# Audio tower on one core: new orders of the segments on all five engines, and a hinted back branch of the main loop

## The chip, the cores and the metric

One core of one Trainium2 chip runs the whole kernel. The metric is the device time of one execution in microseconds (us), lower is better. The kernel before takes 8142.36 us, the median of 3 executions (8140.66 to 8146.43).

## What is computed

For each of 32 sequences of 80,000 samples, the samples are padded and cut into L = 626 frames of 128, and five residual steps follow. All is float32.

```python
h = dct(frames(x))                                  # 626 x 128 per sequence
h = h + mamba_both_ways(layernorm(h))               # scan over time, forward and backward
h = h + moe(layernorm(h))                           # 8 experts, top 2, 128 -> 512 -> 128, gelu
h = h + window_attention(layernorm(h))              # 8 heads of 16, window of 8
h = h + pattern_ffn(layernorm(h))                   # three top-k layers:
#   a1 = gelu(u @ input_patterns.T)   keep top 64 of 512
#   a2 = gelu(kept @ process_in.T)    keep top 128 of 256, softmax, weigh process_values
#   a3 = gelu(agg @ output_in.T)      keep top 64 of 512, weigh output_patterns
```

## The kernel before

**Tiles and stages.** The 626 frames of a sequence are padded to 640, five tiles of 128 partitions. The work is cut into four stages. Stage 1 is the DCT, the first layer norm and the two Mamba directions; stage 2 the mixture of experts; stage 3 the windowed attention; stage 4 the three top-k layers and the output. The stages are pipelined over sequences: while stage 1 works on sequence b, stage 2 works on b-1, stage 3 on b-2 and stage 4 on b-3 (STAGE_LAG).

**The order of the work.** Each engine (TensorE = PE, ScalarE = ACT, VectorE = DVE, GpSimd = POOL, SyncE = SP, which issues DMAs) has a Python generator for each stage, which yields after each segment of instructions. `merged` (L109 to L115) walks a string of digits and emits the next segment of the stage that the digit names. The five strings PE_ORDER, ACT_ORDER, DVE_ORDER, POOL_ORDER and SP_ORDER (L97 to L106) thus fix, by hand, in which order an engine interleaves the four stages:

```python
for digit in order:
    stage = stages[int(digit) - 1]
    if stage is not None:
        next(stage, None)
```

Engines meet through counting semaphores. A segment that waits holds up all that stands behind it on its own engine, of whatever stage. `run` (L353 to L361) emits three ramp-up passes, one hardware loop `engine.Fori(last, NB)` (L358) of 29 iterations whose body is one pass of all four stages, and three ramp-down passes. The loop's branch back is taken 28 times on each engine.

**Stage 1 in the code.** PE transposes x and h, projects the normalized u in 20 half units (L565, into PSUM pS; dA at L562), and for each of 12 units (6 chunks of 105 frames in 2 directions) mixes: C against B (L576), x against its decay (L583), and combines the result with Mt (L593, L599). ACT applies silu to the projections (L847 to L855: Bw, Cs, xs, zs). DVE computes dt (L1046 to L1063), scans the decays (L1071, ab), weighs (L1079 Xw, L1082 Mt), and ends with the variance (L1093) and the scaling of the two directions' outputs into ub_t (L1101). Layer norm moments are L1030 to L1036 on DVE; POOL applies them (L382 rstd, L387 u).

**Stage 2 in the code.** DVE picks the experts (L1114 to L1134) and counts each token's slot (L1139 to L1150). POOL scatters un by slot to routed_rows (L439, L441), SP brings back the rows in 17 tiles of 128 slots. Per tile PE turns the rows (L662), multiplies up (L674, four matmuls) and down (L683, L685), ACT copies the turned rows (L920), applies gelu (L907, four activations), issues the load of a later tile's expert weights (L887) and the store of the answers (L893). POOL gathers the answers (L447, L449), DVE adds them to h (L1157, L1160).

**Stage 3 in the code.** PE q, k, v (L716), DVE products of shifted q and k (L1173 to L1179), ACT exp (L950), POOL and DVE weigh and sum the window by trees of two-input instructions over 128x640 (POOL L459 to L488; DVE L1184, L1188, L1191), and DVE adds to h (L1194, L1198).

**Stage 4 in the code.** POOL copies h into hk (L496). PE computes a1 (L746), transposes the kept (L753, selT), a2 (L761), and so on to the last product (L795, pD); ACT applies gelu (a2 at L970) and copies selT (L967). DVE takes the top 64 of 512 by rounds of MAX8 and MATCH_REPLACE8 (`take_top`, L1218, L1221, closed by L1229), and sorts a2's pairs of halves for the top 128 of 256 (`split_pairs`: L1240 to L1243, then rounds of L1248 and L1251, closed by L1254, L1255; `weigh_pairs` L1265 to L1275). DVE adds the result to hk (L1280); SP stores it (L344, L345).

## Time and profile before

| | before |
|---|---|
| median of 3 executions | 8142.36 us (8140.66 to 8146.43) |
| the profiled execution | 8142.98 us |
| its span in the trace | 8141.2 us |
| granted TensorE clock, mean of the span (share of full speed) | 0.800 |
| DVE busy | 6959.1 us (85% of the span) |
| PE busy | 5529.4 us (68%) |
| ACT, POOL busy | 3232.6 us (40%), 3040.7 us (37%) |
| mean DMA rate | 69 GB/s |

The profiled execution took 8142.98 us, of which the trace's span covers 8141.2 us; it stands 0.62 us above the median. Busy shares are averages over the ramps and the 29 iterations; the iterations repeat closely, so that one of them, read from the loop's first DVE instruction to the next, can be looked at in the place of all.

### The profile page before, as it was taken

To read this page: it belongs to the slowest core of one execution; us is meant where nothing else is said; L and a number is where in the kernel's file an instruction comes from. 1 tells how busy PE (TensorE), PEld (TensorE's weight loads), DVE (VectorE), ACT (ScalarE), POOL (GpSimd) and SP (SyncE) were. 2 spreads that over 40 slices of the span, in tenths; PEclk is the share of its full clock that TensorE was granted. 3 is DMA by queue.
4 is the path that set the end of the run, shared out by engine and by line. 5 is a ranking of instruction groups with operands and counts; after the bars stand their busy time and mean duration, and the time that the engine had idled before them with its cause. 6 is when DMAs were issued, how large, how long until landed. Compare 5 with 4: busy or idle time off the path is not lost.

```text
span 8141.2 us, 109594 instructions
## 1 busy us (share of the span) xinstructions
PE 5529.4 (68%) x31240; PEld 4441.6 (55%) x31240; DVE 6959.1 (85%) x22124; ACT 3232.6 (40%) x7204; POOL 3040.7 (37%) x3192
## 2 busy tenths in 40 slices
PE   6766677776667767667767667767667767667433
PEld 5655555555555555556555556555556555556322
DVE  2378989888989888989888989888989888989887
ACT  2343444433444443344443344433344443344311
POOL 2344443334443433443333443333443333443320
PEclk8887788878788888788877788878788878778755
DMA  2322222222222222222221222222222222222200
GB/s 71 107 79 62 66 85 78 74 65 60 65 85 79 78 62 61 62 85 81 79 64 57 62 84 82 80 62 62 64 77 82 81 65 65 67 67 82 69 2 3
DMA packets 342763, 561.90 MB, mean 69 GB/s; under 512 B 33728, under 2 KB 261792, under 8 KB 341664
## 3 DMA queue, kind: packets, MB, share of 16 engines
q10 hardware_dynamic: 152576, 357.68, 14.2%
q1 hardware_dynamic: 168992, 153.83, 7.3%
q0 software_dynamic: 20480, 41.98, 1.7%
q8 instruction: 311, 5.10, 0.3%
q14 instruction: 404, 3.31, 0.1%
HBM read 484.63 MB, written 68.74 MB: 68 GB/s over the span
## 4 chain that ended last, share of the span: by engine, by line
DVE 67%; PE 9%; issue 8%; DMA 5%; POOL 5%; ACT 3%; ACTq 2%; SPq 1%; DVEq 0%; POOLq 0%
DVE m L1218 15%; DVE work L1221 9%; DVE work L1251 7%; DVE sorted L1248 6%; DVE a L1221 4%; DVE ab L1071 3%; DMA rows<-routed_rows 3%; DVE lg L1173 2%; PE pS L565 2%; PE pD L761 2%; DVE Mt L1082 2%; DMA decay_rows<-dAT 2%; POOL u L387 2%; DVE stats L1030 2%; DVE red L1188 2%
## 5 line engine op out<-in xcount | busy, mean ns | idle before, releaser
L1218 DVE MAX8 m<-work 128x8 f32<-128x512 f32 x1792 | 1143.4, 678 | 1.0
L1221 DVE MATCH_REPLACE8 work<-m,work 128x512 f32<-128x512 f32 x1536 | 1024.8, 674 | 0.0
L565 PE MATMUL pS<-u_fm,wconv_s 128*128 128x315 f32 x3072 | 929.0, 457 | 6.1 <-ACT Cs L849 5.8
L674 PE MATMUL pM<-turned,expert 128*128 128x128 f32 x4352 | 655.2, 297 | 331.7 <-ACT turned L920 327.4
L674 PEld LDWEIGHTS pM<-turned,expert 128*128 128x128 f32 x4352 | 586.0, 206 | 423.6 <-issue 359.9
L565 PEld LDWEIGHTS pS<-u_fm,wconv_s 128*128 128x128 f32 x3072 | 614.2, 205 | 256.3 <-issue 52.8
L907 ACT ACTIVATE hid<-pM,expert 128x128 f32<-128x128 f32 x2176 | 621.2, 370 | 331.6 <-PE pM L674 330.2
L459 POOL TENSOR_TENSOR lg<-lg,red 128x640 f32<-128x640 f32 x256 | 388.5, 1557 | 920.2 <-DVE red L1179 920.2
L685 PE MATMUL pM<-expert,hid 128*128 128x128 f32 x4352 | 672.9, 306 | 0.0
L685 PEld LDWEIGHTS pM<-expert,hid 128*128 128x128 f32 x4352 | 631.6, 223 | 0.0
L599 PE MATMUL pS<-Mt,Xw 121*64 121x121 f32 x3072 | 294.2, 321 | 488.7 <-DVE Mt L1082 486.4
L1251 DVE MATCH_REPLACE8 work<-sorted,work 128x128 f32<-128x128 f32 x2240 | 590.7, 274 | 0.0
L1248 DVE MAX8 sorted<-work 128x8 f32<-128x128 f32 x2560 | 541.0, 277 | 1.1
L1218 DVE MAX8 m<-a 128x8 f32<-128x512 f32 x768 | 503.4, 676 | 40.2 <-issue 34.7
L488 POOL TENSOR_TENSOR lg<-lg 128x640 f32<-128x640 f32 x224 | 363.5, 1647 | 429.7 <-DVE lg L1184 424.7
L1071 DVE TENSOR_TENSOR_SCAN ab<-ab,cst 121x488 f32<-121x488 f32 x384 | 485.1, 1270 | 36.8 <-DMA ab<-decay_rows 36.7
L599 PEld LDWEIGHTS pS<-Mt,Xw 121*64 121x64 f32 x3072 | 189.2, 160 | 585.7 <-DVE Mt L1082 532.9
L998 ACT COPY selT<-pD 128x512 f32<-128x512 f32 x160 | 93.6, 585 | 999.6 <-PE pD L790 999.6
L410 POOL TENSOR_TENSOR yg<-xs,zs 128x525 f32<-128x525 f32 (+1 forms) x256 | 195.3, 796 | 771.6 <-ACT xs L862 763.1
L465 POOL TENSOR_TENSOR red<-lg 128x640 f32<-128x640 f32 x128 | 197.4, 1580 | 741.8 <-ACT lg L950 741.8
L920 ACT COPY turned<-pM 128x256 f32<-128x256 f32 (+1 forms) x544 | 196.2, 361 | 681.9 <-PE pM L685 330.5
L382 POOL TENSOR_TENSOR rstd<-vare,mhalf 128x5 f32<-128x5 f32 x160 | 187.1, 1170 | 624.8 <-DVE vare L1036 624.8
(243 smaller groups left out, 13975.1 us busy)
## 6 DMA issues: line engine op xcount, KB each, us to landing
expert<-in_experts ACTq DMA_DIRECT2D x544, 578.0 KB, 3.9
ab<-decay_rows SPq DMA_DIRECT2D x384, 230.7 KB
rows<-routed_rows SPq DMA_DIRECT2D x128, 256.0 KB, 5.1
answer_rows<-turned ACTq DMA_DIRECT2D x256, 128.0 KB, 4.0
x_sb<-in_x SPq DMA_DIRECT2D x32, 256.0 KB
out<-hk SPq DMA_DIRECT2D x32, 256.0 KB
routed_rows<-un,slot POOLq DMA_INDIRECT x320, 2.8
rows<-answer_rows,slot POOLq DMA_INDIRECT x320, 2.6
```

Of the source, the lines that this page charges most:

```text
L459: last = nc.gpsimd.tensor_tensor(lg[:, w, :], lg[:, w, :], red[:, 0, :], ALU.subtract)
L488: last = nc.gpsimd.tensor_tensor(lg[:, w, :], lg[:, w, :], lg[:, w + n, :], ALU.add)
L565: last = nc.tensor.matmul(pS[:, 512 * (n % 3):512 * (n % 3) + HQ], wt, tap(d, i, half * HQ, HQ), start=(j == 0), stop=(j == len(blocks) - 1))
L599: last = nc.tensor.matmul(pS[r * HD:(r + 1) * HD, B2 + g * WIN:B2 + (g + 1) * WIN], Xw[d][:, hh, :], Mt[d][:, hh, :], start=False, stop=(g ...
L674: last = nc.tensor.matmul(pM[:, bank(i) + j * P:bank(i) + (j + 1) * P], w1_of(i, j), turned[:, (i + 2) % 4, 1, :], start=True, stop=True)
L685: last = nc.tensor.matmul(at, hid[:, i % 2, j, :], w2_of(i, j), start=False, stop=(j == KB - 1))
L907: last = nc.scalar.activation(hid[:, i % 2, j, :], pM[:, at:at + P], ACT.Gelu, bias=b1_of(i, j))
L1071: nc.vector.tensor_tensor_scan(decays, decays, c("scan_src", WIN), 0.0, ALU.mult, ALU.add).then_inc(G["scanned"].s, 1)
L1218: link(nc.vector.max(m8[:, i, :], now[i]), len(tiles) - 1)
L1221: link(nc.vector.match_replace(work[i], m8[:, i, :], now[i], GONE), len(tiles) - 1)
L1248: link(nc.vector.max(top[:, 8 * r:8 * r + 8], left), 2 * n - 1)
L1251: link(nc.vector.match_replace(left, top[:, 8 * r:8 * r + 8], left, GONE), 2 * n - 1)
```

## The change

The five strings of orders are replaced by others with the same count of each digit per string, so no segment is added, dropped or changed, and each engine only takes them in another sequence. The loop is built with a hint of its back branch on each engine: the loop body of each engine begins with one more instruction, which names the branch at its end.

```diff
--- before.py
+++ after.py
@@ -94,16 +94,16 @@
 
 
 
-PE_ORDER = ("14444143433323231111111111214141411134411111111111122424322112211114111111114111112242222122211221211221"
-            "114221111111112114211411112444241414112241111211144142114221412112244144143414434433")
-ACT_ORDER = ("44414334413233121111111113114141421111111111341111424223242112111111111111112424222224224422132221241212"
-             "14424214442144424122144244122421221114424144433")
-DVE_ORDER = ("34244414244211114442444444444434444444411111144444444441111111111433111411114444144444444434444441414343"
-             "42")
-POOL_ORDER = ("321421333333331121113314")
-
-
-SP_ORDER = ("1112221111111213443")
+PE_ORDER = ("44441414112131211114334321111143111131444111111311111341111121122211244212121212211121141111211111212122"
+            "111221121212121211412414114141114211411144142112242424111421212421442144144314344433")
+ACT_ORDER = ("44444111421231413131411131111134111411141411131131231111121124241122212111214211212421244132122221221222"
+             "44144242411444244122424124421222421444124114433")
+DVE_ORDER = ("43441442444141211424424444444414134444144411111444414441144411111411113134414144414444443444444444314344"
+             "12")
+POOL_ORDER = ("123233333331311421331141")
+
+
+SP_ORDER = ("1131221112111213144")
 
 
 def merged(order, *stages):
@@ -355,7 +355,7 @@
             last = max(STAGE_LAG)
             for i in range(last):
                 merged(order, *[stage(engine, i - lag) if i >= lag else None for stage, lag in zip(stages, STAGE_LAG)])
-            with engine.Fori(last, NB) as b:
+            with nc.Fori(last, NB, engines=[engine.engine], hint_back_edge=True) as b:
                 merged(order, *[stage(engine, b - lag) for stage, lag in zip(stages, STAGE_LAG)])
             for i in range(NB, NB + last):
                 merged(order, *[stage(engine, i - lag) if i - lag < NB else None for stage, lag in zip(stages, STAGE_LAG)])
```

**TensorE, the third product a2 of a sequence (L761) and the routed rows (L662).** L761 is stage 4's product of the kept activations selT, in steps of four matmuls; L662 turns stage 2's rows when their DMA has landed; L565 is a projection of stage 1. Before:

```order
L565 MATMUL pS<-u_fm,wconv_s 128x315 x4
L557 REGISTER_ALU
L565 MATMUL pS<-u_fm,wconv_s 128x315 x4
L557 REGISTER_ALU
L565 MATMUL pS<-u_fm,wconv_s 128x315 x4
L661 ISA
L662 MATMUL pM<-cst,rows 128x128 x2
L761 MATMUL pD<-cst,selT 128x256 x4
```

In the change:

```order
L557 REGISTER_ALU
L565 MATMUL pS<-u_fm,cst 128x315
L761 MATMUL pD<-cst,selT 128x256 x4
L753 MATMUL pD<-cst,a 128x128 x4
L761 MATMUL pD<-cst,selT 128x256 x4
L557 REGISTER_ALU
L560 REGISTER_ALU
L562 MATMUL pS<-cst,dtA 128x121
L565 MATMUL pS<-u_fm,cst 128x315
```

The third L761 stood behind the first L662 of a sequence; now the third one stands among projections, ahead of L562 and 25 rows ahead of the first L662.

**TensorE, the first mix of the scan (L576, L583).** L565 is the projection, L674 to L685 is one expert tile of stage 2. Before:

```order
L565 MATMUL pS<-u_fm,cst 128x315
L557 REGISTER_ALU
L565 MATMUL pS<-u_fm,cst 128x315
L557 REGISTER_ALU
L565 MATMUL pS<-u_fm,cst 128x315
L557 REGISTER_ALU
L565 MATMUL pS<-u_fm,cst 128x315
L753 MATMUL pD<-cst,a 128x128 x4
L604 REGISTER_ALU
L576 MATMUL pS<-Cs,Bw 128x121
L583 MATMUL pS<-cst,xs 128x128 x2
```

In the change:

```order
L661 ISA
L662 MATMUL pM<-cst,rows 128x128
L557 REGISTER_ALU
L565 MATMUL pS<-u_fm,cst 128x315
L674 MATMUL pM<-turned,expert 128x128 x4
L681 REGISTER_ALU
L683 MATMUL pM<-expert,cst 128x128
L685 MATMUL pM<-expert,hid 128x128 x4
L662 MATMUL pM<-cst,rows 128x128
L604 REGISTER_ALU
L576 MATMUL pS<-Cs,Bw 128x121
L583 MATMUL pS<-cst,xs 128x128 x2
```

The first mix had three tiles' ups (L674) between the first L662 and itself, and four projections just ahead of it; now it has five, and the last projection stands between two of them.

**VectorE, the end of the loop body.** L1101 scales the scan's output, L1198 ends the attention's residual, L1280 adds stage 4's result to hk, L1157 adds the gathered answers. Before:

```order
L1229 SCALAR_TENSOR_TENSOR a<-a,m 128x512 x2
L1101 SCALAR_TENSOR_TENSOR ub_t<-pS,rstd,ub_t 128x128 x10
L1030 BN_STATS stats<-ub_t 128x6 x5
L1033 BN_AGGR mv<-stats 128x2 x5
L1035 TENSOR_SCALAR nmean<-mv 128x5
L1036 TENSOR_SCALAR vare<-mv 128x5
L1104 ISA
L1194 TENSOR_TENSOR h<-h,pA 128x512
L1279 REGISTER_ALU
L1280 TENSOR_TENSOR hk<-hk,pD 128x128
L1197 REGISTER_ALU
L1198 TENSOR_TENSOR h<-h,pA 128x128
```

In the change:

```order
L1201 ISA
L1279 REGISTER_ALU
L1280 TENSOR_TENSOR hk<-hk,pD 128x128 x2
L1309 ISA
L1101 SCALAR_TENSOR_TENSOR ub_t<-pS,rstd,ub_t 128x128 x10
L1030 BN_STATS stats<-ub_t 128x6 x5
L1033 BN_AGGR mv<-stats 128x2 x5
L1035 TENSOR_SCALAR nmean<-mv 128x5
L1036 TENSOR_SCALAR vare<-mv 128x5
L1104 ISA
L1153 ISA
L1157 SCALAR_TENSOR_TENSOR h<-rows,top,h 128x128 x5
```

L1101 and the moments of ub_t stood ahead of L1194, L1198 and both last L1280; now they stand behind them, just ahead of L1157. On GpSimd the end of the body changes with them: it ended u of ub_t (L382, L387, L424, L427), u of h (L382, L387), hk (L496), h (L431), and now ends u of h, hk (L496), u of ub_t, h (L431).

## Rows read from the trace of the kernel before

**Rows 1.** The page: busy time of the engines; the chain that ended last.
```profile
PE 5529.4 (68%) x31240; PEld 4441.6 (55%) x31240; DVE 6959.1 (85%) x22124; ACT 3232.6 (40%) x7204; POOL 3040.7 (37%) x3192
...
DVE 67%; PE 9%; issue 8%; DMA 5%; POOL 5%; ACT 3%; ACTq 2%; SPq 1%; DVEq 0%; POOLq 0%
```

**Rows 2.** Windows, one iteration: us, busy PE, PEld, DVE, ACT, POOL, clock, DMA, GB/s.
```profile
3164.90:3407.30 242.40, 169.73 (x976) 137.56 (x976) 217.19 (x692) 101.58 (x225) 94.76 (x99) 0.82 0.25 72
```

**Rows 3.** DVE's waits in that iteration: total us, times, longest.
```profile
DVE work L1240 <- ACT a L970: 8.2, 1, 8.2
DVE h L1157 <- POOL hk L496: 6.2, 1, 6.2
DVE stats L1030 <- issue: 3.6, 2, 2.3
DVE Xw L1079 <- PE pS L583: 2.0, 3, 0.9
```

**Rows 4.** DVE's timeline at the loop's head: start, us, then [idle before <- releaser].
```profile
3167.20 0.87 DVE L1030 BATCH_NORM_STATS2 stats<-h 128x6 f32<-128x128 f32 x4 [2.25 <-issue]
3169.47 0.29 DVE L1030 BATCH_NORM_STATS2 stats<-h 128x6 f32<-128x128 f32 x1 [1.39 <-issue]
```

**Rows 5.** Timeline around the third a2, PE and DVE.
```profile
3237.07 0.69 PE L662 MATMUL pM<-cst,rows 128*128 128x128 f32 x2 [6.95 <-DMA rows<-routed_rows]
3237.55 3.62 PE L761 MATMUL pD<-cst,selT 128*128 128x256 f32 x8
...
3241.69 0.56 DVE L1240 TENSOR_TENSOR work<-a 128x384 f32<-128x384 f32 x1 [8.17 <-ACT a L970]
```

**Rows 6.** DVE's timeline: last slot, one sort round of six lists, the first Xw.
```profile
3213.09 0.17 DVE L1150 CAST slot<-slot_f 128x10 int32<-128x10 f32 x1
...
3272.13 1.25 DVE L1248 MAX8 sorted<-work 128x8 f32<-128x128 f32 x6
...
3274.85 1.25 DVE L1248 MAX8 sorted<-work 128x8 f32<-128x128 f32 x6
...
3278.97 0.40 DVE L1079 TENSOR_TENSOR Xw<-pS,dts 121x256 f32<-121x256 f32 x1
```

**Rows 7.** ACT's timeline: a table load, the last silu of the projections, two later tiles' gelu.
```profile
3248.14 1.28 ACT L907 ACT_TABLE_LOAD   x1
...
3256.08 2.03 ACT L855 ACTIVATE zs<-pS 128x315 f32<-128x315 f32 x4 [1.74 <-PE pS L565]
...
3323.18 1.15 ACT L907 ACTIVATE hid<-pM,expert 128x128 f32<-128x128 f32 x4
...
3330.70 1.14 ACT L907 ACTIVATE hid<-pM,expert 128x128 f32<-128x128 f32 x4 [0.72 <-PE pM L674]
```

**Rows 8.** Timeline of the loop's tail, DVE and POOL, and the program's last L1280.
```profile
3146.13 2.80 DVE L1101 SCALAR_TENSOR_TENSOR ub_t<-pS,rstd,ub_t 128x128 f32<-128x128 f32 x10
...
3151.33 0.28 DVE L1280 TENSOR_TENSOR hk<-hk,pD 128x128 f32<-128x128 f32 x1
...
3155.59 0.29 DVE L1280 TENSOR_TENSOR hk<-hk,pD 128x128 f32<-128x128 f32 x1 [1.46 <-PE pD L795]
...
3160.77 1.25 POOL L496 TENSOR_TENSOR hk<-h,zero 128x640 f32<-128x640 f32 x1
...
3162.11 1.14 DVE L1157 SCALAR_TENSOR_TENSOR h<-rows,top,h 128x128 f32<-128x128 f32 x4 [6.23 <-POOL hk L496]
...
8137.68 0.29 DVE L1280 TENSOR_TENSOR hk<-hk,pD 128x128 f32<-128x128 f32 x1 [3.96 <-PE pD L795]
```

**Rows 9.** DVE instructions with two SBUF inputs beside POOL's: timeline, and L1071's min/median/max ns.
```profile
3302.89 1.52 DVE L1254 SCALAR_TENSOR_TENSOR work<-sorted 128x130 f32<-128x130 f32 x1
...
3328.72 2.15 DVE L1071 TENSOR_TENSOR_SCAN ab<-ab,cst 121x488 f32<-121x488 f32 x1
...
L1071 DVE TENSOR_TENSOR_SCAN ab<-ab,cst x384: 1147/1167/2445, 72.1 to 7470.2; 121x488 f32<-121x488 f32 x192
```

**Rows 10.** POOL's timeline: the answers have landed, the gathers can start.
```profile
3369.34 0.19 POOL L447 TENSOR_TENSOR ticks<-zero 128x1 f32<-128x1 f32 x1 [6.25 <-DMA answer_rows<-turned]
```

## The prediction

> **What bounds the kernel now.** I read the page first, then one iteration of the loop. Of the five engines DVE is by far the busiest, 6959.1 us or 85%, with PE next at 68%, and DVE holds 67% of the chain that ended last [rows 1]. An iteration takes 242.40 us, in which DVE is busy 217.19 and PE 169.73 [rows 2]. So the iteration is DVE's instructions plus DVE's waits; an engine other than DVE counts only where DVE waits for it. The list of DVE's waits is therefore the list of what a new order can win: 8.2 us at L1240, 6.2 at L1157, 3.6 at the loop's head under "issue", 2.0 in three pieces at L1079 [rows 3], and 1.5 at L1280 [rows 8]. What each waits for:
>
> L1240 needs the third a2 of stage 4. Its product L761 began at 3237.55, right behind L662, for which PE had stood idle 6.95 us until the routed rows had landed; L761 then took 3.62 us and L1240 began at 3241.69 [rows 5]. A DMA of stage 2 held up stage 4, by nothing but order.
>
> L1157 stands behind hk (L496) on GpSimd, which began at 3160.77 and took 1.25 [rows 8]; hk is free when the last L1280 has been done and stored. The head's 2.25 and 1.39 have no releaser [rows 4]: DVE just passed its branch, so I read them as instructions being fetched.
>
> **The change, part by part.** In each iteration, gains positive. DVE's instructions are the same ones, but for one hint, so only waits and contention can move.
>
> *L1240.* All three L761 now stand ahead of L562 and so of L662. Stage 4's input is there early, since the second L761 was done before the projections ended. The third a2 is then ready before DVE comes to L1240: +8.2.
>
> *The first Xw (L1079).* It is the price of that order. Before, DVE came to it at 3278.97, 111.8 us behind the head at 3167.20 [rows 4, 6]. Off that go the waits ahead of it (8.2 and the head's second 1.4, with 0.3 of small ones): 101.9 of work. In the new DVE order three sort rounds with their closing instructions, which stood ahead of the first scan, stand behind it: a round of six lists takes 3274.85 - 3272.13 = 2.72 [rows 6], so two of those and a shorter one, 7.4 in all. DVE comes to the first Xw at 94.5. When is the product (L583) there? The last slot is cast 3213.09 + 0.17 - 3167.20 = 46.1 behind the head, 44.4 without the waits; two sort rounds of the other group of lists are moved ahead of it (an estimate of 2.5 each, by the same rows), so 49.4. The rows landed 3237.07 - 3213.26 = 23.8 later [rows 5, 6]: 73.2. The first mix now stands behind five ups and four downs of expert tiles, against three and two. On ACT, which alternates gelu and silu, the last four zs ended at 3256.08 + 2.03, 21.0 behind the rows [rows 5, 7]. In the new order ACT has between the rows and its last silu five sets of gelu at 1.14, eight table loads at 1.28, four zs at 0.5 [rows 7], and some fifteen copies, silus and DMA issues of 0.2 to 0.6: 5.7 + 10.2 + 2.0 + 7.3 = 25.2, and some 4 of waits for PE's ups, an estimate by the gap ahead of the second gelu row (0.72 a tile) [rows 7]. That is 29.1, so the product comes at 102.3 and DVE waits 102.3 - 94.5 = 7.8. Bounds: 4 if ACT never waits for PE, 12 if each of four tiles loses another microsecond. I take 7.8: -7.8.
>
> *The back edge.* The hint adds one instruction to each engine's body. Nothing in this trace has a hint, so its price is bounded by the head's rows: from nothing won to all 3.6 won [rows 3]. I take 3.4, near the upper end, because 2.25 and 1.39 are idle time with no releaser that only a late instruction stream explains [rows 4]. The Trainium skill ("Runtime: NRT & Kernel Launch", on instruction fetch mechanics) says that prefetch is purely sequential and a taken branch beyond the pages held forces a fetch; by that rule the 3.6 stays, which is a rival below. +3.4.
>
> *The tail.* Time from the start of L1101 at 3146.13, S, which is when the last selection is done. Before, L1157 began at S + 16.0, with 6.23 + 1.46 of waits in it [rows 8]. In the change L1194, L1093, L1198 and the moments of h come first, and L1280 at S + 3.5. Its second piece came 4.26 behind the first in this row (3155.59 against 3151.33), and waited 3.96 where nothing stood between, at the program's end [rows 8]: S + 7.8, done at S + 8.1. L1101 (2.80) and the moments (1.9) now cover what follows, and L1157 could begin at S + 12.85. hk: at the program's end 8137.97 to 8141.2, 3.2 us, is the store of the last piece; then L496 takes 1.25 [rows 8]: S + 12.6. It is in time. Waits of 7.7 become 4.0: +3.7. If L496 ended as long behind L1280 as now (3162.0 - 3155.9 = 6.1), it would be S + 14.2 and the gain 2.3.
>
> *L1079's small waits.* 2.0 in three [rows 3], where scans follow each other closely. The new DVE order puts rounds between some of them: 2.0 to 0.5, +1.5. Stage 4's softmax, though, now stands behind one more set of gelu on ACT, for which L1265 waits about a third of 1.14 [rows 7]: -0.4.
>
> *Contention.* L1254 on 128x130 took 1.52 us, where a two-input L1280 on 128x128 takes 0.28 [rows 8, 9], and one L1071 took 2.15 where its median is 1.167 [rows 9]; in both cases GpSimd was in a two-input instruction over 128x640 of the attention's trees. That is 2.2 us, of which the new orders part rather over half, by where they put those trees: +1.2, between nothing and 2.2. The Trainium skill ("SBUF — State Buffer", who interferes with whom) says that VectorE with two SBUF inputs and GpSimd reading SBUF exclude each other, whoever came first. The rows agree in direction; by the rule all 2.2 would go only if no pair met at all.
>
> *What is hidden.* The gathers (L447) began 3369.34 - 3167.20 = 202.1 behind the head, 132.3 behind the rows [rows 5, 10]. With the same distance they begin at 205.5 and end their ten issues some 13.6 later, at 219. S lies 3146.13 + 242.40 - 3167.20 = 221.3 behind the head now [rows 2, 4, 8], some 218 in the change. Behind the gathers GpSimd still has u of h, which must start by about S + 6 = 224 for L496 to end in time. That is 5 us of slack, 7 if the tiles go a little faster. Input loads, decay rows and POOL's L382/L387 move within slack larger than that; I cost them at nothing, and the gathers are the first cover that would go.
>
> **Sum.** 8.2 - 7.8 + 3.4 + 3.7 + 1.5 - 0.4 + 1.2 = 9.8 us an iteration, 232.6 instead of 242.4. Times 29 it is 284. The profiled execution took 8142.98, so 7858.8; the median lies 0.6 lower, so 7858. The ramps hold pieces of the same orders, which I put at nothing, within 10 us either way.
>
> **Rivals.**
>
> *B, the first Xw doesn't wait.* If ACT gets its silus done between the tiles, or the rows land sooner, 7.8 come back: 17.6 an iteration, 8142.4 - 510 = 7632. For it: ACT is only 101.58 us busy of 242.40 [rows 2]. Against it: the table loads between gelu and silu, and PE's order, which puts the last projection behind the fourth up. Chance 0.10.
>
> *C, the hint does nothing.* By the rule named above, or because the idle is something else: 6.4 an iteration, 7956. Chance 0.15.
>
> *D, slower.* Expert tiles that share PE with projections and mixes don't go at 5 us each: later tiles began their gelu at 3323.18 and 3330.70, 7.5 apart [rows 7]. With the first gelu 5.2 behind the rows and four tiles at 7.5, the last silu comes at 73.2 + 5.2 + 30 + 2.0 = 110.4, and the first Xw waits 15.9: of 9.8 there remain 1.7. If besides the twelve further tiles each lose 1 us, 12 in all, the gathers pass their slack of 7 by 5, and L1157 waits 5 again: -3.3 an iteration, 8238. It decides from a first wait of 17.6, or from gathers more than 8.7 late. Against it: PE is free for 72 of 242 us [rows 2]. Chance 0.07.
>
> *E, the edits cancel* (the first wait near 17): 8142, chance 0.03.
>
> **Numbers.** Forecast 0.65, B 0.10, C 0.15, D 0.07, E 0.03. The range takes in C, and the forecast's own bounds: a first wait of 4 gives 7748, one of 12 gives 7980, a tail of 2.3 and no contention won 7934. 7740 to 8005 leaves out B, D and E, 0.20. About 0.2% (16 us) is what a measurement can tell here from no change: faster 0.90, same 0.03, slower 0.07.
>
> **What would show it.** DVE's waits of one iteration should read: no L1240; a wait at the first L1079 for PE L583 of 4 to 12 us; "issue" at the head under 0.5; L1280 near 4 and L1157 near nothing; the iteration 232.6. If "issue" still reads 3.6, the hint's term is wrong; if L1157 waits for a DMA of the rows, D's gathers are late; if the first L1079 shows no wait, it is B. DVE busy should be 216.0 in the iteration. The forecast as a whole is wrong if DVE waits more than 18 us in it, or if a line that isn't named here holds over 3.

## The result: 8208 us against 8142, slower by 0.8%

The changed kernel takes 8208.41 us, the median of 4 executions (8200.29 to 8213.67), against 8141.51 (8130.08 to 8146.43) of the kernel before beside it: ratio 1.0083, 95% interval 1.0066 to 1.0101. The forecast was 7858, faster. Nor was it the rival that stood for slower.

The profiled execution took 8208.12 us, span 8206.2, mean granted clock 0.801 (before 0.800). From the page of the profile after, engines' busy time and the chain that ended last, to be read against [rows 1]:

```profile
PE 5716.2 (70%) x31240; PEld 4562.0 (56%) x31240; DVE 7055.1 (86%) x22124; ACT 3365.3 (41%) x7326; POOL 2989.4 (36%) x3192
...
DVE 41%; PE 27%; ACT 16%; issue 8%; POOL 4%; ACTq 2%; DMA 1%; DVEq 0%; SPq 0%; POOLq 0%
```

DVE runs the same 22,124 instructions and is busy 96 us longer. The chain has left it: 67% of it lay on DVE, now 41%, and PE and ACT hold 43%. ACT has 122 more table loads. One iteration, from the head of DVE's loop body to the next, in the windows view (columns as in [rows 2]) and in the list of DVE's waits (total us, times, longest):

```profile
3181.86:3427.64 245.78, 178.46 (x976) 143.17 (x976) 220.37 (x692) 105.97 (x230) 93.09 (x100) 0.81 0.24 70
```

```profile
DVE Xw L1079 <- PE pS L583: 13.4, 2, 12.5
DVE hk L1280 <- PE pD L795: 4.0, 1, 4.0
DVE ab L1071 <- DMA ab<-decay_rows: 2.1, 1, 2.1
DVE a L1265 <- ACT a L983: 1.7, 2, 1.5
DVE lg L1173 <- ACT v L947: 0.8, 1, 0.8
DVE h L1198 <- PE pA L726: 0.5, 1, 0.5
```

Against [rows 3], every wait that the change was to remove is gone: L1240, L1157 and the head's "issue". In their place stands one of 12.5 us at the first L1079. Line by line, gains positive, with the forecast's term behind each:

| us in an iteration | measured | forecast |
|---|---|---|
| L1240 | +8.2 | +8.2 |
| the loop's head | +3.6 | +3.4 |
| the tail: L1157 +6.2, L1280 -2.5 | +3.7 | +3.7 |
| the first L1079 | -12.5 | -7.8 |
| the other L1079 | +1.1 | +1.5 |
| L1265 | -1.7 | -0.4 |
| DVE's busy time (contention) | -3.2 | +1.2 |
| the first scan, L1071, for its decay rows | -2.1 | none |
| L1173 -0.8, small ones +0.3 | -0.5 | none |
| sum | -3.4 | +9.8 |

-3.4 is 242.40 - 245.78. Of the 13.2 us between the two sums, 4.7 are the first L1079, 4.4 the contention, 1.3 L1265, and 2.6 waits for which the forecast had no term; small differences make up the rest. Times 29, -3.4 would be 98 us, and the spans differ by 65.0 (8206.2 and 8141.2): the ramps, and iterations a little unlike these two, gave back some 33, where the forecast had put the ramps at nothing within 10.

**Where the first L1079 lost 4.7.** The slots came exactly when forecast: the last cast ended at 3231.61, 49.4 behind the head at 3182.18. The rows' DMA was issued at 3249.30 and took 7.2 us before (3229.88 to 3237.07), so the rows were there at about 3256.5. Timelines of PE, ACT and DVE, changed kernel:

```profile
3257.84 4.51 PE L565 MATMUL pS<-u_fm,wconv_s 128*128 128x315 f32 x16 [1.11 <-ACT Cs L849]
3262.19 0.27 PE L662 MATMUL pM<-cst,rows 128*128 128x128 f32 x1
```

```profile
3249.53 0.42 ACT L947 COPY v<-pA 128x320 f32<-128x320 f32 x1
3254.80 1.37 ACTq L887 DMA_DIRECT2D expert<-in_experts  x3
3256.29 0.42 ACT L947 COPY v<-pA 128x320 f32<-128x320 f32 x1 [6.34 <-issue]
3262.50 0.27 ACT L925 COPY turned<-pM 128x128 f32<-128x128 f32 x1 [3.75 <-PE pM L662]
```

```profile
3292.06 0.42 DVE L1079 TENSOR_TENSOR Xw<-pS,dts 121x256 f32<-121x256 f32 x1 [12.46 <-PE pS L583]
```

PE did not wait for the rows any more. It came to the first L662 at 3262.19, some 6 us after them. Most of that is PE's own work. The windows from the head to the first L662, before and after (columns as in [rows 2]), show it:

```profile
3167.20:3237.07 69.87, 49.56 (x205) 34.87 (x203) 63.28 (x202) 28.86 (x51) 21.90 (x33) 0.84 0.19 57
3182.18:3262.19 80.01, 59.38 (x237) 43.65 (x238) 75.76 (x233) 31.55 (x54) 25.61 (x38) 0.81 0.17 50
```

PE was busy 9.8 us longer there, since the new order puts more projections (L565) and all three L761 ahead of L662. Without its wait for the rows it would have come 62.9 us behind the head before, and it came at 80.0 now; the other 7 us are waits for GpSimd and ACT (L533 for u, 3.51, is the largest new one). ACT, too, had stood 6.34 us with no releaser: it reads the 17 experts' numbers into registers (L350) and issues three loads. Before, the same segment came early (4.96 us, behind projection 4). But of those 6.34 only 1.11 reached PE, in its wait for Cs (L849); ACT in its turn then waited 3.75 us for PE's L662. From L662 on, the forecast's count holds: the last silu ended 29.1 us behind it, 29.1 was forecast, with the forecast's eight table loads and five sets of gelu. The exact match is in part luck, since ACT's three largest waits in it come to 7.3 us where the forecast had some 4, and its copies to less. The forecast started those 29.1 at the landing of the rows, 73.2 behind the head; they started at 80.0. So the product came 7.6 us later than forecast (109.9 for 102.3), and DVE came to it 2.9 later too (97.4 for 94.5), which leaves the 4.7.

**Where DVE's busy time grew.** Timeline of the changed kernel, DVE, ACT and POOL:

```profile
3311.82 1.68 DVE L1240 TENSOR_TENSOR work<-a 128x256 f32<-128x256 f32 x1
3313.43 1.80 DVE L1241 TENSOR_TENSOR work<-a 128x256 f32<-128x256 f32 x1
3315.26 1.56 DVE L1242 TENSOR_SCALAR work<-work 128x256 f32<-128x256 f32 x1
3316.86 0.42 DVE L1243 TENSOR_REDUCE nmax<-work 128x2 f32<-128x256 f32 x1
```

```profile
3306.99 1.86 DVE L1265 TENSOR_TENSOR_SCAN a<-minus,a 128x256 f32<-128x256 f32 x3 [1.51 <-ACT a L983]
3307.11 4.47 ACT L950 ACTIVATE lg<-lg 128x5120 f32<-128x5120 f32 x1
3311.65 6.61 POOL L465 TENSOR_TENSOR red<-lg 128x640 f32<-128x640 f32 x4 [30.85 <-ACT lg L950]
```

The first three took 0.40, 0.42 and 0.29 us before, on the same shapes; now each takes about as long as one of GpSimd's four instructions beside them (6.61 / 4 = 1.65). The meeting comes from ACT's order. ACT's squares (L983) end at 3306.96. DVE waits for them at L1265 and comes to its second L1240 4.9 us later. ACT takes the attention's exponentials (L950) almost straight behind them, and GpSimd, which waits for those, starts 4.7 us behind the squares. So one event starts both engines, 0.17 us apart at the meeting. Over the run the three lines cost 117 us more, and L1254 34 us less, as the change meant it to. The reduction behind them is not slowed.

### The profile page after: what moved, and what is told of

Same layout as the page of the kernel before. It is cut to its first block, busy times and chain, and to the rows that moved or that the text cites. A ratio compares the mean times of both kernels' runs of the same rounds, so it can differ in the third digit from the quotient of the medians.

```text
span 8206.2 us, 109861 instructions
## 1 busy us (share of the span) xinstructions
PE 5716.2 (70%) x31240; PEld 4562.0 (56%) x31240; DVE 7055.1 (86%) x22124; ACT 3365.3 (41%) x7326; POOL 2989.4 (36%) x3192
## 4 chain that ended last, share of the span: by engine, by line
DVE 41%; PE 27%; ACT 16%; issue 8%; POOL 4%; ACTq 2%; DMA 1%; DVEq 0%; SPq 0%; POOLq 0%
DVE m L1218 12%; PE pS L565 9%; DVE work L1221 8%; PE pD L761 3%; DVE a L1221 3%; PE pM L674 3%; PE pM L685 3%; ACT L907 2%; ACT hid L907 2%; ACT L855 2%; DVE stats L1030 2%; PE pD L795 2%; DVE work L1251 2%; ACTq L887 1%; DVE sorted L1248 1%
## 5 line engine op out<-in xcount | busy, mean ns | idle before, releaser
L1218 DVE MAX8 m<-work 128x8 f32<-128x512 f32 x1792 | 1144.5, 680 | 0.0
L674 PE MATMUL pM<-turned,expert 128*128 128x128 f32 x4352 | 700.9, 314 | 416.1 <-ACT turned L920 413.0
L565 PE MATMUL pS<-u_fm,wconv_s 128*128 128x315 f32 x3072 | 922.3, 451 | 74.5 <-ACT Cs L849 74.5
L674 PEld LDWEIGHTS pM<-turned,expert 128*128 128x128 f32 x4352 | 621.7, 220 | 528.6 <-issue 497.9
L907 ACT ACTIVATE hid<-pM,expert 128x128 f32<-128x128 f32 x2176 | 620.7, 369 | 513.9 <-PE pM L674 511.7
L565 PEld LDWEIGHTS pS<-u_fm,wconv_s 128*128 128x128 f32 x3072 | 600.1, 200 | 330.3 <-ACT Cs L849 104.7
L685 PE MATMUL pM<-expert,hid 128*128 128x128 f32 x4352 | 725.8, 323 | 0.0
L685 PEld LDWEIGHTS pM<-expert,hid 128*128 128x128 f32 x4352 | 686.8, 240 | 0.0
L488 POOL TENSOR_TENSOR lg<-lg 128x640 f32<-128x640 f32 x224 | 340.6, 1545 | 736.1 <-DVE lg L1184 733.4
L1079 DVE TENSOR_TENSOR Xw<-pS,dts 121x256 f32<-121x256 f32 x384 | 157.7, 411 | 504.1 <-PE pS L583 504.1
L1071 DVE TENSOR_TENSOR_SCAN ab<-ab,cst 121x488 f32<-121x488 f32 x384 | 484.8, 1263 | 113.9 <-DMA ab<-decay_rows 113.9
L1218 DVE MAX8 m<-a 128x8 f32<-128x512 f32 x768 | 504.9, 678 | 32.6 <-issue 20.7
L599 PE MATMUL pS<-Mt,Xw 121*64 121x121 f32 x3072 | 271.1, 302 | 290.6 <-DVE Mt L1082 290.6
L998 ACT COPY selT<-pD 128x512 f32<-128x512 f32 x160 | 93.6, 585 | 919.8 <-PE pD L790 919.8
L761 PE MATMUL pD<-cst,selT 128*128 128x256 f32 x1280 | 390.2, 459 | 81.0 <-ACT selT L967 81.0
```

The source lines that it names most:

```text
L488: last = nc.gpsimd.tensor_tensor(lg[:, w, :], lg[:, w, :], lg[:, w + n, :], ALU.add)
L565: last = nc.tensor.matmul(pS[:, 512 * (n % 3):512 * (n % 3) + HQ], wt, tap(d, i, half * HQ, HQ), start=(j == 0), stop=(j == len(blocks) - 1))
L674: last = nc.tensor.matmul(pM[:, bank(i) + j * P:bank(i) + (j + 1) * P], w1_of(i, j), turned[:, (i + 2) % 4, 1, :], start=True, stop=True)
L685: last = nc.tensor.matmul(at, hid[:, i % 2, j, :], w2_of(i, j), start=False, stop=(j == KB - 1))
L761: last = nc.tensor.matmul(pD[:, 512:512 + NP_], selT[:, j * P:(j + 1) * P], pw[:, j, :], start=(j == 0), stop=(j == 3))
L907: last = nc.scalar.activation(hid[:, i % 2, j, :], pM[:, at:at + P], ACT.Gelu, bias=b1_of(i, j))
```

## Experiments

Orders are changed in them, and diffs show the segments of one engine in the sequence in which it takes them ("projection 17" is a half unit of L565, or its silu on ACT; "tile 0" the first expert tile). Each result is a ratio to the kernel before on the same chip, since chips differ: on the five other chips that the runs came to, before takes 8466 to 8517 us.

### The hint alone, and the orders alone

```diff
-            with engine.Fori(last, NB) as b:
+            with nc.Fori(last, NB, engines=[engine.engine], hint_back_edge=True) as b:
```

> The kernel before with the hint of the back branch on all engines and nothing else. Theory: the idle time at the head of VectorE's loop, 3.6 us an iteration, goes and nothing takes its place, so about 108 us less: 8035, 'issue' at L1030 gone. Rival: the wait moves to L1240 or L1157, which end on a DMA or on GpSimd: 8110 to 8141, with L1240 or L1157 longer by up to 3.6.

8409.19 us against 8512.86, ratio 0.9882 (0.9865 to 0.9898): 104 us won, 108 forecast. "Issue" at L1030 is gone and nothing took its place. The page of the profile shows the fetching too: its two queues of kind "instruction" moved 715 packets before and 493 with the hint, in the kernel before as in the changed one, about 8 fewer for each of the 28 branches back. Next, the changed kernel with that line undone:

> The changed kernel with the loop's back branch as it was, without the hint. Theory: the hint is worth the same in either order, so 8208 + 108 = 8316, and the orders alone are slower than before by some 175 us. Rival: in the new orders the first L1079 waits for ScalarE's chain, which absorbs VectorE's idle time at the head: 8208 to 8250, with a shorter wait at L1079.

8430.07, ratio 0.9899 (0.9882 to 0.9916). The orders alone were **faster** than before, where theory and rival had both expected slower. Either the hint costs something in the new orders, or the chip changes the verdict. Both kernels on one chip, the changed one and again the one without the hint:

> The changed kernel once more, beside the kernel before on this chip, because the earlier runs showed another time for the kernel before (8513 us) on another chip. Theory: the ratio belongs to the chip's delays outside the engines (register reads and instruction loading on ScalarE), so on a chip with 8513 for before the changed kernel takes about 8430 - 100 = 8330, ratio 0.98; on one with 8141, 8208, ratio 1.008. Rival: the ratio is the kernel's own, 1.008 everywhere.

> The changed kernel without the hint, the same kernel as before it under another label, beside the changed one on one chip. Theory: 100 us slower than the changed kernel with the hint. Rival: within 20 us of it, because the first L1079 waits for ScalarE anyway.

The changed kernel took 8317.84 against 8466.22, ratio 0.9819 (0.9802 to 0.9835); without the hint 8408.39, ratio 0.9930. So the hint is worth 91 us in the new orders too (85 of it at L1030), and the verdict on the change depends on the chip: 0.8% slower on the one of the result, 1.8% faster here.

### What differs between the chips

> The kernel before, unchanged, for a profile on this chip. Theory: where it takes 8460 to 8520 us instead of 8141, the difference lies in ScalarE, which stops 10 to 12 us without a releaser in each of the two stretches in which GpSimd issues indirect DMAs (L441, L449), and VectorE waits for it at L1240, L1280 and L1093. Rival: it lies in the engines' own busy time or in TensorE's clock.

8464.24 us. DVE's busy time is 6965.2 against 6959.1 [rows 1], so DVE is not slower. PE is busy 5709.8 against 5529.4, at a granted clock of 0.782 against 0.800. The clock is not what makes these chips slow: the changed kernel had 0.807 in after_again and took 110 us longer than on the chip of the result at 0.801. The fetching is not it either: the instruction queues moved the same 715 packets. DVE's waits in this run, and ACT's without a releaser ("remote": the semaphore changed at a moment when no recorded instruction or DMA ended):

```profile
DVE work L1240 <- ACT a L970: 321.2, 30, 13.0
DVE vare L1093 <- PE pS L627: 198.4, 32, 18.7
DVE h L1157 <- POOL hk L496: 192.9, 31, 8.0
DVE Xw L1079 <- PE pS L583: 154.0, 103, 20.9
DVE hk L1280 <- PE pD L795: 139.1, 61, 4.2
```

```profile
ACT xs L852 <- issue: 294.5, 31, 11.7
ACT selT L998 <- remote: 220.6, 26, 9.7
```

On the chip of the result L852 had 156.5 of it and L998 none. DVE's waits account for 310 of the 321 us between the two spans: 81 at L1240, 148 at L1093 and 81 at L1280. The stops end with GpSimd's indirect DMAs. In the changed kernel on such a chip ACT ends a square (L867) and then stands until the last gather is issued. Timelines of that run (after_again), ACT, the last gather of POOL, PE and DVE:

```profile
3444.14 2.43 ACT L867 ACTIVATE zs<-yg 128x1280 f32<-128x1280 f32 x2
3456.78 0.59 ACT L998 COPY selT<-pD 128x512 f32<-128x512 f32 x1 [10.21 <-remote]
```

```profile
3454.78 0.99 POOL L449 DMA_INDIRECT rows<-answer_rows,slot  x1 [0.30 <-issue]
```

```profile
3452.46 1.09 PE L790 MATMUL pD<-cst,a 128*128 128x128 f32 x4 [0.53 <-DVE a L1229]
3453.63 0.47 PE L726 MATMUL pA<-cst,kf 128*128 128x128 f32 x1
```

```profile
3455.36 0.17 DVE L1093 TENSOR_SCALAR vare<-pS 128x10 f32<-128x10 f32 x1 [1.79 <-remote]
3456.81 0.29 DVE L1198 TENSOR_TENSOR h<-h,pA 128x128 f32<-128x128 f32 x1 [1.29 <-remote]
```

ACT moves on 1.0 us behind the last gather's end (1.0 to 1.5 in 24 iterations). It does so because of a semaphore. L998 waits for L790 and DVE's L1198 for L726, both on PE; those matmuls had ended 3.2 and 2.7 us before, by the record, and both engines moved on 0.03 us apart. The trace keeps the times of the semaphores' updates: the one of the last L790 changed at 3456.76, the one of L726 at 3456.79. On the chip of the result each changed within 0.02 us of the recorded end. There ACT waits 7.34 us for the same L790, so of the 10.21 here only 2.9 are the stop. What comes late is the news that PE is done; ACT does not lack its own instructions at that place. With half as many gathers:

```diff
-            for k in range(2 * TILES):
+            for k in range(TILES):
                 nc.gpsimd.indirect_dma_start(rows[:, k, :], None, answers_d, ...
```

> The changed kernel with five gathers (L449) instead of ten, so that GpSimd's stretch of indirect DMAs lasts 6.5 instead of 13 us; it leaves out the answers of the second chosen expert, whose rows keep old data. Theory: on a slower chip ScalarE's stop at L998, which in the changed kernel lasted 10.2 us and ended 1.1 to 1.4 us behind the last gather, ends 6.5 us sooner and lasts some 4 us, again 1 to 2 us behind the last gather. Rival: the stop has nothing to do with the gathers and lasts 10 us.

```profile
ACT selT L998 <- PE pD L790: 920.0, 160, 19.1
```

L998 waits for PE alone, and DVE's L1093 waits 37.2 us in 3, as on the chip of the result (37.4 in 3). Theory and rival are not told apart by the length of the stop: five gathers end some 5 us before L790 does, so a stop that ends 1 to 2 us behind them is covered by the wait for PE. But nothing that ends late is left, and the kernel, without the second expert's answers and in one execution, took 8198.83 against 8470.73 of before, close to what the changed kernel takes on the chip of the result (8208). So what these chips charge the changed kernel hangs on the ten gathers. Why the updates come late there, why one chip has none of it, and whether recording them plays a part, stays open.

The same stops cost the kernel before more, and that gives the reversal: those chips charge the kernel before some 320 us and the changed one 110. At the gathers, L1093 rises by 148 us before and by 87 in the changed kernel, L1280 by 81 and 16. Before, L627, for which L1093 waits, stands behind the late ACT on PE. PE stood 4.97 us in the iteration looked at in before_look, and its granted clock was then 0.50, the lower level (1.2 GHz), for 9 us: the 40 matmuls of L627 took 8.53 us, against 4.71 on the chip of the result, at 0.90. In the new order L627 stands ahead of the last L790. At the scatters (L441), ACT's register reads took 9.5 us on those chips (294.5 in 31), or 11.3 (349.5 in 31, the run with the hint alone), instead of 5.0, worth 81 at L1240. In the changed kernel they lie behind the scatters, 6.5 (200.2 in 31) on the one chip and 6.8 (210.7 in 31) on the other.

### Single moves out of the change

The register reads put back among earlier projections:

```diff
 ACT
+register reads and three expert loads (L350, L887)
 projection 7 ... projection 10, kf, v
-register reads and three expert loads (L350, L887)
 v, projection 11
```

> The changed kernel with one segment of ScalarE moved ahead: the reading of the experts' registers with the first three loads of expert weights (L350, L887) stands before the silu of projection 7 instead of behind projection 10, other orders as changed. Theory: ScalarE loses some 5 us with it in either place, and behind projection 10 it falls right before the routed rows, so that TensorE comes 6 us late to the first L662; moved ahead, part of that hides in ScalarE's waits for TensorE: the first L1079 waits 8 to 10 instead of 12.5, 8070 to 8150. Rival: the wait is set by the alternation of gelu and silu over five expert tiles alone: L1079 waits 12 and more, 8200 or, if the third a2 is late now, 8230.

8561.67, ratio 1.0060 (1.0044 to 1.0077), against 0.98 of the changed kernel on such chips. Worse: the segment then lay in the scatters and took 8.7 us (270.3 in 31 stops at L855), L1240 waited again, 237.6 us in all, and L1079 still 455.7. So on such a chip that place is no better.

The third a2 alone, in the kernel before:

```diff
 PE, ACT
+third a2 (L761 on PE, L970 on ACT)
 first two L662 (L925 on ACT)
-third a2 (L761 on PE, L970 on ACT)
```

> The kernel before with one segment of TensorE and one of ScalarE moved: the third a2 (L761, L970) stands ahead of the two first L662 and L925, without the hint. Theory: the wait at L1240, 8.2 us, goes, and the first L1079, whose product was there some 9 us ahead of need, waits at most 2: 8141 - 200 = 7900 to 7960. Rival: the wait for stage 4 only covered waits behind it, the first L1079 or L1157 takes over: 8060 to 8140.

8459.16, ratio 0.9941 (0.9923 to 0.9959). L1240 kept 227.7 us, so only a part went: here it is mostly ACT's stop in the scatters (L852: 352.6 in 31), not the rows, that holds the third a2. Moving the register reads behind the scatters as well, with the hint:

```diff
 ACT
-register reads and three expert loads (L350, L887)
 projections 5 to 11, selT, third a2
+register reads and three expert loads (L350, L887)
 first L925
```

> The kernel before with the hint, the third a2 ahead of the first routed rows, and ScalarE's register reads and first three expert loads (L350, L887) right before its first L925, where it idles 7 us for the rows, instead of inside the stretch in which GpSimd issues its scatters. Theory: on the slower chips ScalarE stood 10 to 12 us there because nothing it fetches arrives while GpSimd issues indirect DMAs; moved behind the scatters it takes 5 to 7, so L1240's wait goes altogether: ratio to before 0.95 to 0.96 there, 0.96 on a chip with 8141. Rival: the stop belongs to the segment itself, wherever it stands, and the first expert tile comes late by it: 0.98, with L1240 at nothing and a wait at the first L1079.

8508.39, ratio 0.9983 (0.9971 to 0.9994), worse than the hint alone. The segment did take less, 6.7 us (199.9 in 30), and L1240 only 79.3; but the last v (L947) stands behind it, and L1173 waited 361.9 us for that, 12 an iteration. Neither theory nor rival had that wait. The tail of the change in the kernel before, without and with the late register reads:

```diff
 DVE (POOL likewise: u of h and hk ahead of u of ub_t)
-L1093, last round, L1101 and moments of ub_t, L1194, L1280, L1198, L1280, L1157
+last round, L1194, L1093, L1198, L1280, L1280, L1101 and moments of ub_t, L1157
```

> The kernel before with the hint, with the third a2 ahead of the first routed rows (TensorE and ScalarE), and with the changed kernel's tail on VectorE and GpSimd (L1101 and its moments behind L1198 and L1280, hk ahead of u of ub_t; the stage 2 moments two rounds later at the head), all else as before. Theory: the three wins add, 3.6 + 6 + 3.7 = 13 us an iteration, and ScalarE's chain in front of the first mix keeps its place, so the ratio to before is 0.95 to 0.96. Rival: VectorE then runs into waits for ScalarE or TensorE at L1079, L1093 or L1280 that take half of it: 0.975 to 0.985.

> As the one with the late register reads, and with the changed kernel's tail too (VectorE's L1101 and moments behind L1198 and L1280, GpSimd's hk ahead of u of ub_t, the transposed x behind three of the first products at the head on TensorE and ScalarE so that nothing stands behind GpSimd there). Theory: 3.7 us an iteration more is won at L1157: ratio 0.94 to 0.95. Rival: the waits reappear at L1198, L1280 and at the head as in the earlier run with the tail, no gain over the late register reads alone.

8363.32, ratio 0.9889 (0.9862 to 0.9915), and 8369.84, ratio 0.9823 (0.9806 to 0.9839). The first missed by a head where PE's transposes of x waited for GpSimd's u, with the products for L1218 behind them (159.5 us at L1218); the second, with that mended, shows the tail's worth over the late reads: 1.6%, 139 us, 4.8 an iteration. The theory had 3.7 for it, the rival nothing.

### Where the first L1079 comes from

> The changed kernel with VectorE's slots of the routed rows (L1139 to L1150) one sort round earlier, so that the rows are there 2.5 us sooner. Theory: the rows were not what TensorE and ScalarE waited for, they came late to them because of the projections, so the first L1079 waits as in the changed kernel, 12 to 13 us an iteration once its place 2.5 us earlier is counted in, and the time is within 30 us of the changed kernel. Rival, the forecast's own model: the first product comes a fixed distance behind the rows, so L1079 waits 2.5 us less and the kernel is 70 us faster than the changed one.

```diff
 DVE
-first and second round of the second group, slots (L1139 to L1150)
+first round of the second group, slots (L1139 to L1150), second round
```

8411.25, ratio 0.9874 (0.9857 to 0.9890), not faster than the changed kernel's 0.9819 (another chip of the same kind). The time alone does not decide, since L1240 now waits 61.9 us. The wait at L1079 does: it is 511.7 us, 507.5 in after_again, where the forecast's model wants some 70 less. Rows that come 2.5 us sooner win nothing there: a first product at a fixed distance behind the rows is refuted. Now the chain behind L662 itself:

```diff
 PE
 L662, projection 16, L662
+projections 17 to 19
-up 0, up 1, projection 17, down 0, up 2, down 1, projection 18, up 3, down 2, projection 19, up 4, down 3, mix 0
+up 0, up 1, down 0, up 2, down 1, mix 0, up 3, down 2, up 4, down 3
 ACT
+projections 15 to 19
-gelu 0, projection 15, gelu 1, gelu 2, projections 16, 17, gelu 3, projection 18, gelu 4, projection 19
+gelu 0, gelu 1, gelu 2, gelu 3, gelu 4
```

> The changed kernel with the last projections (L565 17 to 19 on TensorE, their silus 15 to 19 on ScalarE) taken ahead of the first expert tile instead of between the first five, and the first mix behind the third up, so that ScalarE changes between gelu and silu 3 times less each way. Theory: the first L1079 waits under 3 us instead of 12.5, but the expert tiles start some 7 us later and save 6 of table loads, and the gathers had only 4 us to spare, so that some 4 us an iteration is won, 100 us less than the changed kernel, with a new wait at L1101 for GpSimd. Rival: the full 9 to 12 us is won, 300 us less. Second rival: nothing, since the tiles' delay comes back at the gathers in full.

> The changed kernel with the last projections ahead of the first expert tile, once more, beside the next one. Theory: ratio to before 0.95 where before takes 8460 to 8520; where it takes 8141, the changed kernel's 1.008 less 261/8141, so 0.976. Rival: 0.98 or more, if the earlier run owed its gain to its chip.

8102.27, ratio 0.9511 (0.9495 to 0.9526), and 8069.15 on another chip, 0.9533 (0.9510 to 0.9556). Waits of DVE in the first of them:

```profile
DVE a L1265 <- ACT a L983: 211.4, 52, 7.8
DVE hk L1280 <- PE pD L795: 143.7, 62, 4.0
DVE Xw L1079 <- PE pS L583: 140.1, 55, 22.7
```

L1079 fell from 507.5 to 140.1. Between 600 and 7500 us, in the iterations, it fell from 370.1 to 37.1; the ramps hold the rest. The win over the changed kernel is 3%, 9 us an iteration, more than the theory's 4. ACT saves three table loads each way, 187 at L907 becoming 92. But 5 us came up at L1265, as ACT's marks stand behind five tiles. Moving those:

```diff
 PE
 down 3
+fifth a2 (L761)
 up 5, second mix
-fifth a2 (L761)
 ACT
 kept tile 3, fifth a2
+marks, exponentials and squares of the first group (L976, L979, L983)
 gelu 5, first y (L862), kept tile 4
-marks, exponentials and squares of the first group (L976, L979, L983)
```

> As the one with the last projections ahead of the first tile, and ScalarE's marks and exponentials of stage 4 (L976 to L983) ahead of the sixth set of gelu instead of behind the fifth kept tile, with the fifth a2 (L761) ahead of the sixth up on TensorE. Theory: the wait at L1265, some 5 us an iteration there, goes to under 1, two more table loads cost ScalarE 2.6 us that nobody waits for: 100 to 130 us less than without that move. Rival: it delays y of the first units and the expert tiles, and the wait moves to L1079 or behind the gathers: no gain.

8035.54 beside n_proj2's 8069.15: ratio 0.9488 (0.9467 to 0.9510). 34 us, a third of the theory. L1265 has 98.9, but L1079 302.6: the rival. DVE's busy time fell to 6963.7, with the 117 us at L1240 to L1242 back: the squares (L983) no longer stand just ahead of the attention's exponentials on ACT, which undid the meeting with GpSimd. And with the first y ahead of the squares:

```diff
 ACT
 marks and exponentials
+first y (L862)
 squares, gelu 5
-first y (L862)
```

> As the one with ScalarE's marks moved ahead, but with the first y (L862) between the marks with exponentials (L976, L979) and the squares (L983), instead of behind both and a set of gelu. Theory: the second mix's L583 waited 5.7 us for that y, and VectorE's L1079 behind it; both go to about 2, and 3 to 4 us an iteration are won over that run, ratio to before 0.935 to 0.94. Rival: the wait moves to L1265 or to the second scans, ratio 0.945 to 0.95 as there.

7961.1 against 8513.84, ratio **0.9350** (0.9334 to 0.9365), as its theory had it. L1079 is down to 195.2. This kernel beats both, on such a chip by 6.5% and 4.8%.

### The contention by itself

```diff
 ACT
-exponentials of the attention (L950), gelu 6, third y, kept tile 5, gelu 7, kept tile 6
+gelu 6, third y, kept tile 5, gelu 7, kept tile 6, exponentials of the attention (L950)
```

> The changed kernel with ScalarE's exponentials of the attention (L950) moved back behind the next copy of an expert tile (L920), so that GpSimd's sums behind them begin some 8 us later, after VectorE's second L1240 to L1242. Theory: those three take 1.3 us instead of 5.0, so 100 us less than the changed kernel unless other pairs meet. Rival: the pairing only moves to other VectorE instructions with two inputs (L1265, L1254, L1071), within 30 us of the changed kernel.

8378.32, ratio 0.9899 (0.9878 to 0.9920), slower than the changed kernel beside it (0.9819). L1240 to L1242 gave back 117.5 us, but L1265's scans took 48.5 more, L1071 28.9 and L1254 13.4, and the wait at L1265 grew by 60. The rival's mechanism held, though not its 30 us: GpSimd's long stretch met the next instructions with two inputs, and the kernel lost 60 us.

The wait at the first L1079 is not what makes the pairs meet. In n_proj no L1079 of the iterations waits longer than 1.9 us, and yet the meeting is the same, 0.17 us apart, and L1240 to L1242 take 203.7 us over the run (205.5 in the result's trace). One iteration of n_proj, ACT, POOL and DVE:

```profile
3257.65 4.47 ACT L950 ACTIVATE lg<-lg 128x5120 f32<-128x5120 f32 x1
3262.19 6.54 POOL L465 TENSOR_TENSOR red<-lg 128x640 f32<-128x640 f32 x4 [24.42 <-ACT lg L950]
3262.36 1.67 DVE L1240 TENSOR_TENSOR work<-a 128x256 f32<-128x256 f32 x1
```

## Why the prediction was wrong

**The reading of before was right.** DVE's waits were all to be had: L1240, the head and the tail came out at 8.2, 3.6 and 3.7, forecast 8.2, 3.4 and 3.7, and the times of the tail fit (L1157 at S + 12.6, forecast 12.85, with hk done 0.35 us before it).

**The first Xw is the step that failed.** The sum took "73.2", the landing of the rows, for the moment at which PE comes to L662, because PE had waited there before. In the new order it was PE that came late, at 80.0. The forecast counted neither PE's work ahead of L662, which grew from 49.6 to 59.4 us, nor ACT's, where the register reads and two projections now stand just ahead of the rows; the first is the larger part, the second cost PE 1.1. The 29.1 behind L662 was right in its sum; n_rows shows that the rows did not bind, n_proj that the chain of silus and table loads behind L662 did. The product came 7.6 late, DVE itself 2.9, and the wait was 12.5 for 7.8, just outside the forecast's own bounds of 4 to 12.

**Contention had the wrong sign, and weighs as much.** "+1.2" was -3.2. Either of the two terms as forecast would have left the sum near +1 us an iteration, and neither alone gives the 9.8. The forecast parted the old pairs (L1254 did win 34 us) and did not look for new ones. The new pair could have been read from the strings: ACT's exponentials stand just behind the squares for which DVE waits. The Trainium skill ("SBUF — State Buffer", who interferes with whom) has `tensor_scalar`, in the modes that use both ports, among the VectorE instructions that can share a port with GpSimd, and `tensor_reduce` among those that never do on trn2. The trace agrees in that L1242 went from 0.29 to 1.56 us and L1243 stayed at 0.42; whether L1242 runs in such a mode, no run here shows.

**Terms left out.** The first scan waited 2.1 for its decay rows and L1173 0.8 for v; the prediction had "decay rows ... within slack larger than that" and "at nothing", because they were early before. L1265 was mis-sized, 1.7 for 0.4. The forecast's own sign of being wrong came true: it named more than 18 us of waits in the iteration, and DVE waits 22.5.

**The rivals.** C, no gain by the hint, is refuted by two pairs of runs: 104 and 91 us. By the Trainium skill ("Runtime: NRT & Kernel Launch", instruction fetch mechanics) a taken branch out of the pages held makes the engine wait for a fetch; the unhinted runs agree (3.6 us at the head with no releaser, and the instruction packets above), and the hint takes that wait away. B and E are out. D named the right place and put its threshold for slower at a first wait of 17.6 or late gathers; slower came with 12.5, through contention and small waits that D had not counted. The gathers began 218.5 behind the head, 13 later than forecast, but the end of the selections moved by nearly as much, and L1157 did not wait for them.

What stays open: what differs in the chips, and what the single moves, all of them run on the slower chips, and n_y0 take on one like that of the result.

## What to carry to other kernels

When an order is changed so that a resource no longer waits for an event, the event stops being the clock of what follows. Count again from the engine that now comes last, with everything that the change put ahead of it there, its own work first. For contention, look for pairs of engines that one event starts: their distance is fixed by the order, whatever waits come before. Where the pairs can't be read, leave the term at zero with both signs in the range. And where two chips run the same kernel 4% apart, compare only on one chip, and say which.

## What the runs showed of the hardware

A hint of the back branch took away 3.6 us an iteration at the head of VectorE's loop, and as much at TensorE's (L527: 105.1 us in 29 waits before, 9.9 in 9 with the hint alone), with 222 packets fewer on the instruction queues.

On five of six chips, while GpSimd issued ten indirect DMAs, the news that a matmul of TensorE was done came late to the engines that waited for it. In 24 iterations of after_again ScalarE and VectorE moved on 1.7 to 3.7 us behind the recorded ends (0.04 on the sixth chip), together, and 1.0 to 1.5 us behind the last issue; with five DMAs VectorE's share of these waits was gone. ScalarE's register reads took 9.5 to 11.4 us in such a stretch, 5.0 on the sixth chip. The same source was 0.8% slower on one chip and 1.8% faster on another.

Three VectorE instructions over 128x256 beside GpSimd's 128x640, one of them a `tensor_scalar` with a single input, took 1.6 to 1.8 us instead of 0.3 to 0.4; a `tensor_reduce` was not slowed.
